# An attention and FFN block on one core: half of the output weight's remainder on GpSimd, the cross-chunk product in three products of halves

## The reference

```python
q = rope(h @ Wq.T); k = rope(h @ Wk.T); v = h @ Wv.T      # 32 heads, 8, 8
dt = softplus(h @ Win.T + dt_bias);  g = -dt * exp(A_log_bias)
G = cumsum(g) within a chunk of 128 tokens (two chunks per sequence)
y_intra = ((q k^T) * exp(G_i - G_j) * causal) @ (v * dt)
state   = (k * exp(Glast - G))^T @ (v * dt)                 # of the chunk before
y_inter = (q * exp(G)) @ state
y = (y_intra + y_inter) / rms * gnorm_w * silu(h @ Wg.T)
x = x + ga * (y @ Wo.T);   then the FFN (512 -> 1376 -> 512)
```

## Time and profile before

| | us |
|---|---|
| median of 3 runs | 1114.43 (1110.83 to 1117.56) |
| the profiled execution | 1111.14 |
| its span | 1109.4 |
| TensorE busy | 1053.0 (95%) |
| VectorE busy | 822.3 (74%) |
| ScalarE busy | 693.4 (63%) |
| GpSimd busy | 205.9 (19%) |

### The profile page before, as it was taken

One profiled execution on the slowest core, in us unless ns is written; L12 is line 12 of the kernel. 1 busy time (PEld: TensorE's weight loads), 2 busy tenths in 40 slices (PEclk: granted clock), 3 DMA queues, 4 the chain that ended last, 5 costly groups with the idle time before them and its releaser, 6 DMA issues. The chain is left out here.

```text
span 1109.4 us, 14573 instructions
## 1 busy us (share of the span) xinstructions
PE 1053.0 (95%) x4680; PEld 806.0 (73%) x4680; DVE 822.3 (74%) x1585; ACT 693.4 (63%) x1360; POOL 205.9 (19%) x131
## 2 busy tenths in 40 slices
PE   5889999999999999999999999999998859999898
PEld 1657777777777777777777777777775339888786
DVE  5777887888788788878888887888778785434411
ACT  3447877787778778777877787787775334222300
POOL 3411211112221112111122111121112430000000
PEclk9989999999999999999999999999999879999999
DMA  6122401210131123012201310240033222111011
GB/s 224 58 67 61 126 20 38 82 69 19 38 113 38 25 59 123 19 38 88 63 19 38 113 38 28 61 120 19 19 96 134 76 98 74 55 39 57 29 38 38
DMA packets 37464, 70.89 MB, mean 64 GB/s; under 512 B 2936, under 2 KB 19576, under 8 KB 35520
## 3 DMA queue, kind: packets, MB, share of 16 engines
q1 hardware_dynamic: 36720, 70.16, 20.0%
q10 hardware_dynamic: 720, 0.43, 0.1%
HBM read 68.33 MB, written 2.24 MB: 64 GB/s over the span
## 5 line engine op out<-in xcount | busy, mean ns | idle before, releaser
L1357 POOL TENSOR_TENSOR q_sin<-q_sin,cst 128x512 f32<-128x512 f32 x64 | 88.8, 1388 | 311.4 <-ACT q_sin L758 311.4
L1350 POOL TENSOR_TENSOR dec<-dec,future 128x1024 f32<-128x1024 f32 x31 | 74.4, 2401 | 342.3 <-ACT expg L777 342.3
L54 PE MATMUL ps_q<-hT_hi,wq_hi 128*128 128x512 f32 x256 | 125.4, 490 | 3.4 <-DVE q_cos L1012 2.5
L1202 DVE SCALAR_TENSOR_TENSOR prob<-ps_s,scal,dec 128x128 f32<-128x128 f32 x256 | 72.0, 344 | 59.0 <-PE ps_s L664 58.8
L54 PE MATMUL ps_o<-wo_hi,z_hi 128*128 128x512 f32 x260 | 105.1, 404 | 6.2 <-DVE z_lo L49 5.7
L54 PE MATMUL ps_gt<-hT_hi,wg_hi 128*128 128x512 f32 x256 | 103.6, 405 | 2.1 <-DVE sg L1032 2.1
L56 PE MATMUL ps_o<-wo_hi,z_lo 128*128 128x512 f32 x260 | 103.8, 399 | 0.0
L55 PE MATMUL ps_o<-wo_lo,z_hi 128*128 128x512 f32 x260 | 103.4, 398 | 0.0
L56 PE MATMUL ps_q<-hT_hi,wq_lo 128*128 128x512 f32 x256 | 101.2, 395 | 0.0
L55 PE MATMUL ps_gt<-hT_lo,wg_hi 128*128 128x512 f32 x256 | 101.0, 394 | 0.0
L56 PE MATMUL ps_gt<-hT_hi,wg_lo 128*128 128x512 f32 x256 | 100.9, 394 | 0.0
(11 more groups left out here) (248 smaller groups left out, 2720.1 us busy)
## 6 DMA issues: line engine op xcount, KB each, us to landing
dec<-gT_dram SPq DMA_DIRECT2D x32, 512.0 KB, 5.4
raw_q<-wq_in SPq DMA_DIRECT2D x32, 256.0 KB, 2.6
raw_g<-wg_in SPq DMA_DIRECT2D x32, 256.0 KB, 2.9
raw_o<-wo_in SPq DMA_DIRECT2D x8, 1024.0 KB, 7.3
raw_pair<-wkv_in SPq DMA_DIRECT2D x8, 512.0 KB, 4.4
raw_pair<-wgu_in SPq DMA_DIRECT2D x6, 512.0 KB, 3.3
raw_gu<-wgu_in SPq DMA_DIRECT2D x5, 512.0 KB, 3.3
qT<-wmod_in SPq DMA_DIRECT2D x2, 1024.0 KB, 6.9
```

Source lines behind the costliest of these rows:

```text
L54: pe.matmul(out, w_hi, x_hi, start=first, stop=False)
L1202: last = nc.vector.scalar_tensor_tensor(prob[:, h], ps_s[:, h * P:(h + 1) * P], scal[:, tile, 1, h:h + 1], dec[:, tile // 2 % 2, h, tile % ...
L1350: nc.gpsimd.tensor_tensor(cells, cells, future[:].unsqueeze(1).broadcast_to([P, GRP * CPB, CHUNK]), ALU.add).then_inc(mask_done, 1)
L1357: nc.gpsimd.tensor_tensor(q2, q2, sinT, ALU.mult).then_inc(qsin_done, 1)
```

## The change

The cross product of an odd step is made by three products of halves. ScalarE makes `cross_hi` in even steps behind `round_squares`, and VectorE makes `cross_lo` behind `gated_y` (in the last four steps both are VectorE's). The plain copy `v` is no longer made. `cross_lo` lies in the memory of `cross`, and `prob_lo` in that of `prob` (`whole_and_rest`). The output weight is handled in two halves: heads 0 and 1 as before; for heads 2 and 3 ScalarE rounds behind `exp_gate` of step 0, and GpSimd makes the remainder. TensorE waits for the second half at its third head, and SyncE before it loads anew.

```diff
--- before.py
+++ after.py
@@ -205,6 +205,11 @@
         def sem(name):
             return ctx.enter_context(nc.semaphore(name))
 
+        def whole_and_rest(name):
+
+            at = nc.sbuf_base
+            whole = sb(name, [P, GRP, CHUNK])
+            return whole, nc.alloc_sbuf_tensor_at(name + "_lo", [P, GRP, CHUNK], F32R, offset=at)
 
         wq_hi, wq_lo = (sb(n, [P, GRP, KT, D], F32R) for n in ("wq_hi", "wq_lo"))
         wg_hi, wg_lo = (sb(n, [P, GRP, KT, D], F32R) for n in ("wg_hi", "wg_lo"))
@@ -222,15 +227,16 @@
         scal = sb("scal", [P, NT, 3, GRP])
 
         kr = sb("kr", [P, CPB, D])
-        v = sb("v", [P, 2, D])
         v_hi, v_lo = sb("v_hi", [P, 2, CPB, D], F32R), sb("v_lo", [P, 2, CPB, D], F32R)
-        cross = sb("cross", [P, GRP, CHUNK])
-
-
-        prob, z = sb("prob", [P, GRP, CHUNK]), sb("z", [P, GRP, CHUNK])
+        cross, cross_lo = whole_and_rest("cross")
+        cross_hi = sb("cross_hi", [P, GRP, CHUNK], F32R)
+
+
+        z = sb("z", [P, GRP, CHUNK])
         sq_parts = sb("sq_parts", [P, HALF], F32R)
         sq_top, sq_sum = sb("sq_top", [P // 2, HALF]), sb("sq_sum", [P // 2, HALF])
-        prob_hi, prob_lo = (sb(n, [P, GRP, CHUNK], F32R) for n in ("prob_hi", "prob_lo"))
+        prob, prob_lo = whole_and_rest("prob")
+        prob_hi = sb("prob_hi", [P, GRP, CHUNK], F32R)
         rms = sb("rms", [P, HALF])
         z_hi, z_lo = sb("z_hi", [P, GRP, CHUNK], F32R), sb("z_lo", [P, GRP, CHUNK], F32R)
         sig = sb("sig", [P, HALF])
@@ -298,6 +304,8 @@
         kv_hi_done = sem("kv_hi_done")
         kv_split = sem("kv_split")
         wo_hi_done = sem("wo_hi_done")
+        wo_late_hi = sem("wo_late_hi")
+        wo_late = sem("wo_late")
         wo_split = sem("wo_split")
         q_ready = sem("q_ready")
         g_ready = sem("g_ready")
@@ -326,6 +334,8 @@
         mask_done = sem("mask_done")
         dec_done = sem("dec_done")
         cross_done = sem("cross_done")
+        xhi_done = sem("xhi_done")
+        xlo_done = sem("xlo_done")
         vlo_done = sem("vlo_done")
         phi_done = sem("phi_done")
         plo_done = sem("plo_done")
@@ -472,6 +482,7 @@
                     load_head(g + 1, t)
                 if next_group and t == 1:
                     sp.wait_ge(wo_split, g + 2)
+                    sp.wait_ge(wo_late, g + 2)
                     load_o(g + 1)
                 if next_group and t == 2:
                     sp.wait_ge(kv_split, g + 1)
@@ -479,6 +490,7 @@
 
                 if not next_group and t == 1:
                     sp.wait_ge(wo_split, KVH + 1)
+                    sp.wait_ge(wo_late, KVH + 1)
                     load_mod(GA)
                     load_mod(GB)
 
@@ -568,6 +580,8 @@
                 if t <= 1:
                     pe.wait_ge(wo_split, g + (t + 1))
                 for h in range(GRP):
+                    if h == 2 and t <= 1:
+                        pe.wait_ge(wo_late, g + (t + 1))
                     last = three_products(nc.tensor, ps_o[:], z_hi[:, h], z_lo[:, h],
                                           wo_hi[:, h], wo_lo[:, h], h == 0, h == GRP - 1)
                 last.then_inc(o_ready, 1)
@@ -669,9 +683,11 @@
 
                 b, c = t // 2, t % 2
                 if c == 1:
-                    pe.wait_ge(cross_done, g * 4 + (b + 1))
-                    nc.tensor.matmul(ps_y[:], v[:, b % 2], cross[:].rearrange("p h i -> p (h i)"),
-                                     start=True, stop=False)
+                    pe.wait_ge(xlo_done, g * 4 + (b + 1))
+                    pe.wait_ge(vlo_done, g * 4 + (b + 1))
+                    three_products(nc.tensor, ps_y[:], v_hi[:, b % 2, 0], v_lo[:, b % 2, 0],
+                                   cross_hi[:].rearrange("p h i -> p (h i)"),
+                                   cross_lo[:].rearrange("p h i -> p (h i)"), True, False)
                 pe.wait_ge(vlo_done, g * 4 + (b + 1))
                 pe.wait_ge(phi_done, g * 8 + (t + 1))
                 p_hi, p_lo = (p[:].rearrange("p h i -> p (h i)") for p in (prob_hi, prob_lo))
@@ -791,7 +807,6 @@
             def copy_v(g, b):
                 act.wait_ge(kv_ready, g * 4 + (b + 2))
                 ps_v = ps_kv[:].rearrange("p (c d) -> p c d", c=CPB)[:, :, D:2 * D]
-                nc.scalar.activation(v[:, (b + 1) % 2], ps_v[:, 0], ACT.Copy)
                 nc.scalar.activation(v_hi[:, (b + 1) % 2], ps_v, ACT.Copy).then_inc(v_done, 1)
 
             def round_squares(g, t):
@@ -880,7 +895,14 @@
 
                 act.wait_ge(o_ready, g * 8 + 1)
                 act.wait_ge(wo_loaded, g * 16 + 16)
-                nc.scalar.activation(wo_hi[:], raw_o[:], ACT.Copy).then_inc(wo_hi_done, 1)
+                nc.scalar.activation(wo_hi[:, 0:2], raw_o[:, 0:2], ACT.Copy).then_inc(wo_hi_done, 1)
+
+            def split_late_o_hi(g):
+                nc.scalar.activation(wo_hi[:, 2:4], raw_o[:, 2:4], ACT.Copy).then_inc(wo_late_hi, 1)
+
+            def split_cross_hi(g, b):
+                act.wait_ge(cross_done, g * 4 + (b + 1))
+                nc.scalar.activation(cross_hi[:], cross[:], ACT.Copy).then_inc(xhi_done, 1)
 
             def split_prob_hi(g, t):
                 act.wait_ge(prob_done, g * 8 + (t + 1))
@@ -899,12 +921,16 @@
                 if next_group and t == GRP + 1:
                     split_kv_hi(g + 1)
                 round_squares(g, t)
+                if c == 0:
+                    split_cross_hi(g, b)
                 if c == 1:
                     copy_kT(g, b)
                 decays(g, t + 1)
                 if t == 0:
                     split_o_hi(g)
                 exp_gate(g, t)
+                if t == 0:
+                    split_late_o_hi(g)
                 if c == 0:
                     sigmoid(g, t)
                     copy_v(g, b)
@@ -973,7 +999,7 @@
 
             def split_o_lo(g):
                 dve.wait_ge(wo_hi_done, g + 1)
-                split_lo(nc.vector, wo_lo[:], raw_o[:], wo_hi[:]).then_inc(wo_split, 1)
+                split_lo(nc.vector, wo_lo[:, 0:2], raw_o[:, 0:2], wo_hi[:, 0:2]).then_inc(wo_split, 1)
 
             def copy_scalars(g, b, first=False):
 
@@ -1230,6 +1256,14 @@
                 dve.wait_ge(sqhi_done, g * 8 + (t + 1))
                 split_lo(nc.vector, sq_parts[64:128], sq_sum[:], sq_parts[0:64]).then_inc(sqlo_done, 1)
 
+            def split_cross_lo(g, t, tail=False):
+                b = t // 2
+                if tail:
+                    dve.wait_ge(cross_done, g * 4 + (b + 1))
+                    split_hi(nc.vector, cross_hi[:], cross[:]).then_inc(xhi_done, 1)
+                dve.wait_ge(xhi_done, g * 4 + (b + 1))
+                split_lo(nc.vector, cross_lo[:], cross[:], cross_hi[:]).then_inc(xlo_done, 1)
+
             def split_prob_lo(g, t, tail=False):
                 if tail:
                     dve.wait_ge(prob_done, g * 8 + (t + 1))
@@ -1262,6 +1296,8 @@
                 sum_squares(g, t)
                 rotate_q_add(g, t)
                 gated_y(g, t)
+                if c == 0:
+                    split_cross_lo(g, t)
                 add_out(g, t)
                 if heads:
                     split_head_lo_g(g + 1, t - 1)
@@ -1291,6 +1327,7 @@
                 gated_y(g, t)
                 if c == 0:
                     cross_probabilities(g, t)
+                    split_cross_lo(g, t, True)
                 if t == 4:
                     copy_scalars(g, b)
                 if t < NT - 1 and t != 5:
@@ -1351,6 +1388,11 @@
                                         future[:].unsqueeze(1).broadcast_to([P, GRP * CPB, CHUNK]),
                                         ALU.add).then_inc(mask_done, 1)
 
+            def split_late_o(g):
+
+                pool.wait_ge(wo_late_hi, g + 1)
+                split_lo(nc.gpsimd, wo_lo[:, 2:4], raw_o[:, 2:4], wo_hi[:, 2:4]).then_inc(wo_late, 1)
+
             def rotate_q_sin(g, t):
                 pool.wait_ge(swap_done, g * 8 + (t + 5))
                 q2 = q_sin[:].rearrange("p (b i) -> p b i", b=2)
@@ -1361,7 +1403,8 @@
             nc.gpsimd.memset(ones[:].bitcast(F32), 1.0).then_inc(ones_done, 1)
 
             nc.gpsimd.memset(wo_hi[:].bitcast(F32), 0.0)
-            nc.gpsimd.memset(wo_lo[:].bitcast(F32), 0.0).then_inc(wo_split, 1)
+            nc.gpsimd.memset(wo_lo[:, 0:2].bitcast(F32), 0.0).then_inc(wo_split, 1)
+            nc.gpsimd.memset(wo_lo[:, 2:4].bitcast(F32), 0.0).then_inc(wo_late, 1)
             nc.gpsimd.memset(z_hi[:].bitcast(F32), 0.0).then_inc(zhi_done, 1)
             nc.gpsimd.memset(z_lo[:].bitcast(F32), 0.0).then_inc(zlo_done, 1)
             pool.wait_ge(future_done, 1)
@@ -1382,6 +1425,8 @@
                 b, c = t // 2, t % 2
                 if project:
                     rotate_q_sin(g, t)
+                if t == 0:
+                    split_late_o(g)
                 if c == 0 and next_batch:
                     mask(g, b)
 
```

## The result

The changed kernel takes 1109.18 us (median of 19 runs, 1107.29 to 1110.33), the kernel before beside it 1114.07 (19 runs). The ratio is 0.9954, 95% interval 0.9944 to 0.9963: 0.46% faster, just inside the 0.5% that I had called no change. The profiled execution took 1108.23 us with a span of 1106.3, 3.1 us less than before's 1109.4.

A forecast was written before the change was run, and what follows sets the result against it. Bounds: TensorE in 6/7, a late chain at 0/1, a VectorE and ScalarE loop in 2/3 and 4/5. Groups -5.7, last group -1.7, last steps 0: -7.4 gives 1103.7 or 1107.0 by starting point; forecast 1105 us, range 1096 to 1113.

The forecast's parts named there:

- the boundary 0/1: Passage from step 0 to 1 of a group, where a late ScalarE and VectorE chain holds TensorE; 1.55 us less.
- The 1.32 us of waiting for `z_lo`: Step 1's first output product waits on VectorE, 2.87 us after the cross product against 1.55; claimed gone.
- the pair's 1.55 us: Steps 0 and 1: the next scores come at S0+25.20 instead of S0+26.75 (S0: start of step 0's scores).
- The main reading: Steps 2/3 and 4/5: a VectorE and ScalarE loop of 24.95 us has no slack, so added work shows.
- the pairs 2/3 and 4/5: Loop gains 0.61 us (cross remainder), loses 0.16 (copy of `v`): 25.40 instead of 24.95, 0.45 more each.
- the 7.58 us: Steps 2/3 and 4/5: time given from `z` to the end of the squares' remainder.
- Pair 6/7: Steps 6 and 7 of a group: TensorE sets the pace, so its cheaper cross product saves 0.17 us.
- The step that failed: Last group's last four steps: VectorE's added cross work hides in existing waits; 0 us, bounds -0.3 and +4.4.
- The second rival: Gain given back: loop costs 0.9 us per pair or the last steps pay 4.4; 1108 to 1113; chance 0.22.
- my sum of -7.4: Whole kernel: seven groups -5.7 us and the last group's first four steps -1.7, together -7.4.
- The first (the pairs hide the remainder): Steps 2/3 and 4/5 have slack, each other pair saves 0.17 us: 16.1 less, about 1096; chance 0.10.
- The third (GpSimd in front of `cap`): Step 0: GpSimd's weight half starts before `cap`, `z` at S0+18.7; about +10 us, 1121; chance 0.08.

The follow-up runs named there:

- e11_half_first: The full change, but ScalarE rounds the second half of the output weight ahead of the gate's exponential; span 1130.1 us, ratio 1.0149 against the kernel before.

## Why the prediction was right, and where it was not

*The direction and the place were right*: the loop got 6.6 us shorter (forecast 7.4), through the boundary 0/1 alone; in the change's second trace 5.0, since the loop's first step was long. The 1.32 us of waiting for `z_lo` are gone, and the pair's 1.55 us came out as 1.52 in the group of the table. The weight's part alone (99.9 us a group) and the cross part alone (102.8) show where it comes from.

*The main reading was right*: the pairs 2/3 and 4/5 are paced by the loop over VectorE and ScalarE. Forecast 0.45 us more each, measured 0.44 and 0.43. Adding 0.16 us on ScalarE added 0.16 to the pair, taking 0.61 off VectorE took 0.57 and 0.60 off them, down to TensorE's own length. One reading beside it was misworded: the 7.58 us run from `z` to the start of the squares' remainder (129.21), not to its end; the sum doesn't change.

*Terms that were off.* "Pair 6/7: TensorE-bound, so 0.17 less": it was 0.01 less. The square sum came 0.14 earlier, but the next group's first scores started 0.33 us after it instead of 0.23. Where no turn of the loop follows, after the seventh group and in the last group's step 3, it is 0.23 again and the pair has 24.81. What the turn waits for wasn't tried. That is 0.16 us in a group, the difference between 100.8 and 100.9.

*The step that failed* is the last four steps: "The new work fits into that wait [...] I take 0; bounds -0.3 and +4.4". They were 3.2 us longer in the first pair of traces and 2.9 in the second. I had looked at the cast of `prob`, which did wait less (0.43 instead of 2.28 us), and not at the copy of the scalars ahead of it, which the two additions pushed into the mask. That made the values of step 5 1.5 us late in both pairs, 1.2 of it through the copy's place. The rest of the 3.2 is not shown to be the change's: the same last steps as before took up to 2.8 us more in the trace of the weight's part alone, by the meeting at `kr` and by the granted clock.

*How near the number came.* The second rival (given back in the last steps, 0.22) is nearest to what happened, on top of my forecast's loop: 6.6 us gained there and 3.2 returned in the traces, 0.46% in the timed runs. From the later median of before, 1114.07, my sum of -7.4 gives 1106.7 and not 1105, which started from a point between the profiled execution and the median of three; measured is 1109.18. I gave "faster by over 0.5%" 0.57 and "same" 0.34; the measured value is on the side of the second, by a few hundredths of a percent. The range held it.

*The other rivals.* The first (the pairs hide the remainder) fell: 25.4 us, not 24.8. The third (GpSimd in front of `cap`) did not come about in the change, its price for a group was right: `z` at S0+18.68 against 18.7, a group 1.5 us above before's against 1.4; for the whole kernel it was too low, a span of 1130 against about 1121. Three products cost 0.68 us, so the change does on TensorE what it says.

*The rule weighed.* That an instruction of VectorE stands until GpSimd's is over was seen on `cap`, on the scalars' copy, on `kr`, `prob_lo` and the cast. The Trainium skill's "SBUF — State Buffer", section "SBUF: two separate sides", states such a lock for some VectorE instructions, among them those with two SBUF inputs against a GpSimd instruction that reads SBUF, and says that whichever starts first keeps it. The traces agree: `kr` and `prob_lo` have two SBUF inputs and waited, the `prob` products with one input in PSUM did not (1.11 us in all four beside a scaling). e11_half_first shows which order costs 2 us.

## What to carry to other kernels

Close the loops over the helping engines before trusting a full TensorE: where the links from an instruction to itself a period later were all work or handoff, 0.16 and 0.45 us added to them came out as 0.16 and 0.44, and what was saved on TensorE was not gained. Test the halves of a change apart; here one half was worth 1.2% and the other cost more than half of it. Take a second trace of both kernels before explaining 2 or 3 us of a single stretch. When work is put ahead of something on VectorE, look for the GpSimd instruction that the thing behind it will now meet, down to the smallest copy.

## What the runs showed of the hardware that I had not expected

A VectorE copy of 24 columns, 0.17 us alone, took 2.34 us beside a GpSimd instruction, in five traces of five, while the four `prob` products, which read PSUM and SBUF, kept their 1.12 us (1.11 beside GpSimd's scaling). When a VectorE and a GpSimd instruction started in the same hundredth of a microsecond, at `kr`, either could be the long one: `kr` took 0.43 us and the scaling 1.55 in one trace, 1.54 and 1.25 in another of the same program. And in e11_half_first gaps of 2 us in all between TensorE's products in step 1 were followed by products 0.43 us apart instead of 0.23 in two groups of eight, and not in the others.
